# GRU steps 64 to 495 as PE loops, with the products beside them in fp16

## The reference, cut to what matters

```python
def cell(h, x):                       # 512 steps, one after the other; h is 4 x 512
    gi = x @ W_ih + b_ih              # does not depend on h
    gh = h @ W_hh + b_hh
    i_r, i_z, i_n = jnp.split(gi, 3, axis=-1)
    h_r, h_z, h_n = jnp.split(gh, 3, axis=-1)
    r = jax.nn.sigmoid(i_r + h_r)
    z = jax.nn.sigmoid(i_z + h_z)
    n = jnp.tanh(i_n + r * h_n)
    h_new = (1.0 - z) * n + z * h
    return (h_new, h_new)
...
x = x + _L2_cond_ref(cond_2048, x, L2_cond_W_ih, L2_cond_W_hh, L2_cond_b_ih, L2_cond_b_hh)
x = x + _L3_cond_ref(x, cond_2048, 1, 1)   # each row of x, interpolated at 512 places given by cond
```

## Time and profile before

| | |
|---|---|
| median of 3 runs | 2281.44 us (2278.91 to 2283.96) |
| the profiled execution | 2288.73 us |
| its span, first to last instruction | 2286.8 us |
| busy: PE, DVE, ACT, POOL | 2172.7, 1563.6, 1207.0, 504.3 us |
| steps 64 to 495 begin, end | 952.74, 2228.05 us |
| granted clock in steps 64 to 495 | 1.00 |

### The profile page before, as it was taken

One profiled execution on the slowest core, in us unless ns is written; L12 is line 12 of the kernel. 1 busy time (PEld: TensorE's weight loads), 2 busy tenths in 40 slices (PEclk: granted clock), 3 DMA queues, 4 the chain that ended last, 5 costly groups with the idle time before them and its releaser, 6 DMA issues.

```text
span 2286.8 us, 130730 instructions
## 1 busy us (share of the span) xinstructions
PE 2172.7 (95%) x56269; PEld 1831.7 (80%) x56269; DVE 1563.6 (68%) x6093; ACT 1207.0 (53%) x5574; POOL 504.3 (22%) x2271
## 2 busy tenths in 40 slices
PE   5768999999989999999999999999999999999998
PEld 3654655545545999999999999999999999999997
DVE  7987968869687466666666666666666667666665
ACT  6765947759467344566444444444444444444443
POOL 2002121021211122233222222222222222222222
PEclk8569999999999999999999999999999999999999
DMA  5000000010010000000000000000000000000000
GB/s 204 3 2 1 1 1 1 1 56 1 1 56 1 22 5 5 5 5 5 5 5 9 5 9 10 5 9 5 9 10 5 10 5 9 10 5 14 12 10 15
DMA packets 8715, 31.51 MB, mean 14 GB/s; under 512 B 1028, under 2 KB 1352, under 8 KB 7880
## 3 DMA queue, kind: packets, MB, share of 16 engines
q1 hardware_dynamic: 7712, 23.07, 2.7%
q10 hardware_dynamic: 424, 0.07, 0.0%
HBM read 18.94 MB, written 4.19 MB: 10 GB/s over the span
## 4 chain that ended last, share of the span: by engine, by line
PE 81%; DVE 12%; ACT 4%; issue 2%; DMA 1%; POOL 0%; SPq 0%; DVEq 0%; POOLq 0%; ACTq 0%
PE psum L1924 53%; PE psum L1832 9%; PE psum L1735 3%; PE psum L1656 3%; PE psum L1698 2%; PE psum L1753 2%; PE psum L1859 2%; PE psum L1719 2%; DVE region_cols L1087 2%; DVE region_cols L1103 2%; DVE top L1280 2%; ACT region_rows L751 1%; PE psum L1675 1%; DMA region_cols<-in_L_cond_W_emb_dram 1%; PE psum L1872 1%
## 5 line engine op out<-in xcount | busy, mean ns | idle before, releaser
L1924 PE MATMUL psum<-partsA,region_w_hh 128*128 128x40 f16 x24576 | 858.2, 179 | 7.2 <-issue 1.7
L1924 PE MATMUL psum<-partsB,region_w_hh 128*128 128x40 f16 x24576 | 858.2, 179 | 2.4 <-issue 1.9
L1924 PEld LDWEIGHTS psum<-partsA,region_w_hh 128*128 128x128 f16 x24576 | 761.7, 96 | 82.2 <-DVE partsA L1499 11.3
L1924 PEld LDWEIGHTS psum<-partsB,region_w_hh 128*128 128x128 f16 x24576 | 726.7, 95 | 5.4 <-issue 3.8
L564 POOL TENSOR_TENSOR region_w_b<-region_w_b 128x16 f32<-128x16 f32 x1022 | 242.6, 237 | 1135.5 <-DVE region_w_b L1488 1135.5
L1462 DVE TENSOR_REDUCE psum<-psum 128x8 f32<-128x32 f32 x1024 | 201.2, 197 | 292.5 <-PE psum L1924 291.3
L916 ACT ACTIVATE mixA<-psum 128x8 f32<-128x8 f32 x512 | 94.7, 185 | 549.7 <-DVE psum L1462 549.7
L930 ACT ACTIVATE region_w_b<-psum 128x8 f32<-128x8 f32 x1024 | 189.3, 185 | 151.2 <-DVE psum L1477 94.1
L1832 PE MATMUL psum<-region_cols,region_w_a 128*128 128x256 f32 (+1 forms) x864 | 252.7, 390 | 1.0 <-DVE region_cols L1269 0.9
L1488 DVE TENSOR_TENSOR_SCAN region_w_b<-giveB,region_w_b 128x40 f32<-128x40 f32 x512 | 123.6, 241 | 128.5 <-ACT region_w_b L930 128.5
L566 POOL COPY region_work<-region_w_b 128x8 f32<-128x8 f32 x1024 | 203.5, 199 | 2.2 <-DVE region_w_b L1488 2.2
(11 more groups left out here) (234 smaller groups left out, 2590.3 us busy)
## 6 DMA issues: line engine op xcount, KB each, us to landing
region_rows<-in_x_dram SPq DMA_DIRECT2D x4, 1024.0 KB, 11.1
region_w_a<-in_L_cond_W_qkv_dram SPq DMA_DIRECT2D x1, 3072.0 KB, 22.9
region_w_hh<-in_L_cond_W_hh_dram SPq DMA_DIRECT2D x4, 768.0 KB, 6.5
region_w_a<-in_L_cond_W_ih_dram SPq DMA_DIRECT2D x1, 3072.0 KB, 10.2
out_dram<-region_w_b SPq DMA_DIRECT2D x12, 256.0 KB, 3.1
region_cond<-in_cond_dram SPq DMA_DIRECT2D x2, 1024.0 KB, 7.9
region_cols<-in_L_cond_W_emb_dram SPq DMA_DIRECT2D x1, 2048.0 KB, 19.4
region_w_out<-in_L_cond_W_out_dram SPq DMA_DIRECT2D x1, 1024.0 KB, 21.5
```

Source lines behind the costliest of these rows:

```text
L1924: made = e.matmul(k.slots(bank)[:, :, ch, :, 0:2], k.w16[:, 2 * read + c, part, NC * "rzn".index(g) + 2 * half + ch], k.parts[read][:, c]. ...
```

## The change

From step 64 on, PE's code is a loop over steps (`Fori`) for each stretch of 8, 16 or 48 steps of one kind: 23 loops, each aligned to a block of 256 instructions. Inside, the values that semaphores must reach are registers, and the four side matmuls of a turn find their operands by register addresses, which `lower_ap` works out ahead of the units `BAr` and `ABz`.

Each side operand is split into two fp16 parts, as the state is: `w_parts` and `x_parts` for the gates, `x3_parts` and `sampling` for the rows. One fp32 matmul of 256 columns becomes four fp16 matmuls of 256 columns. ACT makes each high part and DVE the low one, in steps given by tables (`W_STEPS`, `X_STEPS`, `HAT_STEPS`, `X3_STEPS` and others), after DVE has found scales of 2 from the largest weights and inputs (`dve_input_most` in steps 0 to 27, `dve_input_scale` in 28 to 33). POOL's addition of the diagonal to the hats goes to DVE.

All groups of the loops go to one bank, with products that always add to what is there; ACT takes a group after its last turn and then writes zeros into the bank (`act_clear`), and PE waits for `cleared` before each turn's side products. PE no longer waits for `zsum` and `nline`. The gates of steps 0 to 127 stay in fp32.

```diff
-    for i in range(ROW_GROUPS * B):
-        plan.append((LATE_PRODUCTS + NC * i, [("late", i)], 1))
...
+def loop_groups():
+
+    groups = []
+    for q in range(2, CHUNKS):
+        s = STARTS[q]
+        if q + 1 < CHUNKS:
+            groups += [("gates", s + NC * j, q + 1, j) for j in range(12)]
+            s += 12 * NC
+        if q > 2:
+            groups += [("rows", s + NC * i, 4 * (q - 3) + turn) for i, turn in enumerate(ROW_TURNS)]
+    for second in range(2):
+        groups += [("late", LATE_PRODUCTS + NC * (4 * second + i), 4 * second + turn) for i, turn in enumerate(ROW_TURNS)]
+    return groups
+
+
+LOOPED = STARTS[2]
+LOOP_GROUPS = loop_groups()
+LOOP_GROUP_AT = {group[1]: n for n, group in enumerate(LOOP_GROUPS)}
+TAKE_STEPS = {group[1] + NC - 1: n for n, group in enumerate(LOOP_GROUPS)}
+CLEARED = [group[1] + NC for group in LOOP_GROUPS]
...
+def act_take_looped(e, k, n):
+    s = k.sem
+    kind, _, *args = LOOP_GROUPS[n]
+    e.wait_ge(s["side_products"], NC * (n + 1))
+    if kind == "gates":
+        act_take_gates(e, k, *args, SIDE_BANK[0], None)
+    elif kind == "rows":
+        act_take_rows(e, k, *args, SIDE_BANK[0])
+    else:
+        act_take_late_rows(e, k, *args, SIDE_BANK[0])
+
+
+def act_clear(e, k, n):
+    s = k.sem
+    kind, _, *args = LOOP_GROUPS[n - 1] if n else ("gates", 0, 2, 10)
+    if kind == "gates":
+        e.wait_ge(s["gates_in"], 12 * args[0] + args[1] + 1)
+    else:
+        e.wait_ge(s["rows_out"], ROWS_TAKEN[n - 1])
+    e.activation(k.bank(SIDE_BANK[0], HALF_ROW), k.zero[:].broadcast_to([P, HALF_ROW]),
+                 ACT.Copy).then_inc(s["cleared"], CLEARED[n] - (CLEARED[n - 1] if n else 0))
...
+        if st in TAKE_STEPS:
+            act_take_looped(e, k, TAKE_STEPS[st])
+            if TAKE_STEPS[st] + 1 < len(LOOP_GROUPS):
+                act_clear(e, k, TAKE_STEPS[st] + 1)
+        if st == LOOPED - 4:
+            act_clear(e, k, 0)
+        if st in W_STEPS:
+            act_weight_high(e, k, W_STEPS[st])
+        if st in X_STEPS:
+            act_input_high(e, k, *X_STEPS[st])
+        if st in AWAY_STEPS:
+            act_away(e, k, AWAY_STEPS[st])
         if st in HAT_STEPS:
             act_hat(e, k, HAT_STEPS[st])
+        if st in HAT_HIGH_STEPS:
+            act_hat_high(e, k, HAT_HIGH_STEPS[st])
+        if st in X3_STEPS:
+            act_x3_high(e, k, X3_STEPS[st])
...
+def dve_input_low(e, k, q, c):
+    s = k.sem
+    e.wait_ge(s["x_halved"], NC * (q - FIRST_HALVED) + c + 1)
+    e.scalar_tensor_tensor(k.x_parts[:, q % 2, 1, c], k.xT[:, c, :, STARTS[q]:STARTS[q] + LONG], k.in_scale[:, 1:2],
+                           k.x_parts[:, q % 2, 0, c], ALU.mult, ALU.subtract).then_inc(s["x_lowered"], 1)
...
+        if st < MOST_PIECES:
+            dve_input_most(e, k, st)
+        if SCALE_AT <= st < SCALE_AT + len(SCALE_OPS):
+            dve_input_scale(e, k, st - SCALE_AT)
+        if st - 1 in W_STEPS:
+            dve_weight_low(e, k, W_STEPS[st - 1])
         if st in PLACE_STEPS:
             dve_place(e, k, PLACE_STEPS[st])
+        if st in X_LOW_STEPS:
+            dve_input_low(e, k, *X_LOW_STEPS[st])
+        if st in DIAGONAL_STEPS:
+            dve_diagonal(e, k, DIAGONAL_STEPS[st])
+        if st in HAT_LOW_STEPS:
+            dve_hat_low(e, k, *HAT_LOW_STEPS[st])
         if st in ADDS:
             dve_add_states(e, k, *ADDS[st])
+        if st in X3_LOW_STEPS:
+            dve_x3_low(e, k, *X3_LOW_STEPS[st])
+        if st in NEXT_LOW_STEPS:
+            dve_next_low(e, k, NEXT_LOW_STEPS[st])
...
+            dve_last_low(e, k, c - 1)
+    dve_last_low(e, k, NC - 1)
...
+def pe_four_batches(e, k, bank, parts, part, c):
+
+    for low in range(2):
+        for sampled in range(2):
             for b in range(B):
-                made = e.matmul(k.bank(part, HALF_ROW)[32 * b:32 * b + 32], k.xT[:, c, b, rows],
-                                k.sampling[:, b, c, part * HALF_ROW:(part + 1) * HALF_ROW],
-                                start=(c == 0), stop=(c == NC - 1), tile_position=(0, 32 * b))
-        made.then_inc(s["last_rows"], 1)
+                made = e.matmul(k.bank(bank, HALF_ROW)[32 * b:32 * b + 32], parts[:, c, low, b],
+                                k.sampling[:, part, b, c, sampled],
+                                start=(c == low == sampled == 0), stop=(c == NC - 1 and low == sampled == 1), tile_position=(0, 32 * b))
+    return made
...
+    for st in range(LOOPED):
+        pe_step(e, k, st)
+        pe_side(e, k, st)
+    for q in range(2, CHUNKS):
+        at = STARTS[q]
+        if q + 1 < CHUNKS:
+            pe_gate_loop(e, k, q + 1)
+            at += 12 * NC
+        if q == 2:
+            pe_free_loop(e, k, at, STARTS[3])
+        else:
+            tile, second = divmod(q - 3, 2)
+            for half in range(ROW_GROUPS):
+                pe_row_loop(e, k, at + 2 * NC * half, B * tile + 2 * second, half)
+    for second, half in itertools.product(range(2), range(ROW_GROUPS)):
+        pe_row_loop(e, k, LATE_PRODUCTS + 2 * NC * (2 * second + half), B * (NT - 1) + 2 * second, half)
+    for st in range(NEXT_PRODUCTS, S):
+        pe_step(e, k, st)
+        pe_side(e, k, st)
...
+def pe_gate_loop(e, k, q):
+    s = k.sem
+    first = STARTS[q - 1]
+    w_parts = k.w_parts.rearrange("p j c l n -> p (j c l n)")
+    x_parts = k.x_parts[:, q % 2].rearrange("p l c b n -> p (l c b n)")
+    if q > FIRST_HALVED:
+        e.wait_ge(s["x_lowered"], NC * (q - FIRST_HALVED + 1))
+    e.addr_align(PE_BLOCK, max_nops=4)
+    with e.Fori(0, 12 * NC) as turn:
+        weights = [w_parts[:, bass.ds(turn * (2 * P) + low * P, P)] for low in range(2)]
+        moving = [x_parts[:, bass.ds(turn % NC * HALF_ROW + low * NC * HALF_ROW, HALF_ROW)] for low in range(2)]
+        count = e.compute_val(turn + (first + 1))
+        e.compute_val(turn % NC)
+        pe_looped_step(e, k, count, weights, moving)
+        if q == FIRST_HALVED:
+            e.wait_ge(s["w_lowered"], W_PIECES)
+            e.wait_ge(s["x_lowered"], NC)
+        pe_looped_products(e, k, count, weights, moving)
...
+    sampling = k.sampling[:, half, b:b + 2].rearrange("p b c l n -> p (b c l n)")
+    e.wait_ge(s["x3_lowered"], 2 * (u + 2))
+    e.wait_ge(s["hat_lowered"], 2 * NC * (b + 2))
+    e.addr_align(PE_BLOCK, max_nops=4)
+    with e.Fori(0, 2 * NC) as turn:
+        weights = [x3_parts[:, bass.ds(turn * (2 * P) + low * P, P)] for low in range(2)]
+        moving = [sampling[:, bass.ds(turn * (2 * HALF_ROW) + low * HALF_ROW, HALF_ROW)] for low in range(2)]
+        count = e.compute_val(turn + (first + 1))
+        pe_looped_step(e, k, count, weights, moving)
+        pe_looped_products(e, k, count, weights, moving)
...
+def pe_looped_step(e, k, count, weights, moving):
+    for u in GRU_UNITS:
+        if u == "BAr":
+            e.lower_ap(weights[0], for_matmul_weights=True)
+            e.lower_ap(moving[0])
+        if u == "ABz":
+            e.lower_ap(weights[1], for_matmul_weights=True)
+            e.lower_ap(moving[1])
+        pe_unit(e, k, u, count)
+
+
+def pe_looped_products(e, k, count, weights, moving):
+    s = k.sem
+    to = k.bank(SIDE_BANK[0], HALF_ROW)
+    e.wait_ge(s["cleared"], count)
+    for stationary in weights:
+        for columns in moving:
+            made = e.matmul(to, stationary, columns, start=False, stop=True, skip_group_check=True)
+    made.then_inc(s["side_products"], 1)
...
+    if u in ("AAr", "BAr"):
+        e.wait_ge(s[f"low{u[0]}"], count)
+    if u in ("AAr", "ABr"):
+        e.wait_ge(s[f"put{h}"], count)
```

More of the change, by code:

```diff
@@ L140 @@
 SIDE = side_table()
-BANK_USE = [("gates", 0, j) for j in range(12)] + [group for _, groups, _ in side_plan() for group in groups]
 def side_done(s):
     return [(group, number % 2) for group, number, part in SIDE.get(s, ()) if part[-1] == NC - 1]
-FREE = [st for st in range(2 * LONG) if st >= LONG and not side_done(st)]
-PLACE_STEPS = {st: i for i, st in enumerate(range(44, 44 + 3 * B))}
-HAT_STEPS = {st: i for i, st in enumerate(FREE[:2 * B * NC])}
-def add_table():
[L156 to L165, removed]
+FIRST_HALVED = 3
@@ new lines, in pe_free_loop @@
+def pe_free_loop(e, k, first, end):
+    e.addr_align(PE_BLOCK, max_nops=4)
+    with e.Fori(first + 1, end + 1) as count:
+        for u in GRU_UNITS:
+            pe_unit(e, k, u, count)
[7 more added lines that the diff above has]
+            e.lower_ap(moving[1])
+        pe_unit(e, k, u, count)
@@ new lines, in pe_step, with pe_unit @@
+def pe_step(e, k, st):
+    s = k.sem
+    if st == 0:
+        e.wait_ge(s["gru_first"], 16)
+        e.wait_ge(s["w_kept"], NC)
+        e.wait_ge(s["w_low"], NC)
+    for u in GRU_UNITS:
+        pe_unit(e, k, u, st + 1)
+def pe_unit(e, k, u, count):
+    s = k.sem
+    read, h, g = "AB".index(u[0]), u[1], u[2]
+    half = "AB".index(h)
+    bank = {"r": R_BANK, "z": Z_BANK, "n": N_BANK}[g][half]
+    if u in ("AAr", "BAr"):
+        e.wait_ge(s[f"low{u[0]}"], count)
```

(22 more changed lines are left out.)

377 lines of the change are left out of this document (242 added, 135 removed).

## The result

The changed kernel takes 2250.21 us (median of 4 runs, 2247.79 to 2251.07) against 2282.7 us before (4 runs, 2278.91 to 2288.22): ratio 0.9854, 95% interval 0.9832 to 0.9876. That is 32.5 us less where 41 were forecast; the forecast of 2240 was 10 us too low.

A forecast was written before the change was run, and what follows sets the result against it. PE was taken to set the step's pace, near a 2.805 us floor. 33 + 14.5 saved less 5 + 1 + 1 makes 41 us: profiled 2288.73 to 2248, median 2240; own range 2223 to 2260, overall 2222 to 2348.

The forecast's parts named there:

- Side products: In 416 steps, four fp16 matmuls replace one fp32 matmul on PE: step 2.923 to 2.84 us, 33 us saved.
- Instruction fetch: In steps 64 to 495, PE's waits for the next code block vanish because loops stay within one block: 14.5 us saved.
- Entries: PE entering each of 23 loops in a new code block: 0.2 us each, 5 us given back, range 0 to 23.
- Loop control: PE's added waits, register computations and branch in each turn: hidden behind queued work, costing nothing.
- Rival A: PE's sequencer becomes the bound: at 80 ns an instruction, 108 us over 432 turns, giving 2348 us; chance 0.18.
- the cluster: About 14 control instructions around a loop's end on PE: 0.71 us at 51 ns each, hidden by 0.87 us.
- Rival B: The backward branch drops the code block, so every turn fetches again: 86 us, giving 2326 us; chance 0.08.
- Clear: ACT's zeroing of 256 columns behind the take in 104 steps: fits its 1.20 us gap, cost 0; 10 us if doubled.
- halves' work: ACT's fp16 copies and DVE's low parts fit idle gaps; with the input search in steps 0 to 27, 1 us.
- The end: After the recurrent steps, the last sums gain a pass through ACT and DVE before PE may start: 1 us added.

The follow-up runs named there:

- written-out code: The changed kernel with its 23 loops written out, constant addresses and waits, fp16 side matmuls kept: 2281.8 us, ratio 1.0007 to the kernel before.
- the loop of four blocks: The changed kernel with four steps in each loop turn instead of one, about 840 instructions: 2288.13 us, ratio 1.0026 to the kernel before.

## Why the prediction came out right, and 10 us low

- *Side products*, 33 us: right. 416 x (2.923 - 2.842) = 33.7 us in loops. What the sum did not say is that they gain nothing in written-out code.
- *Instruction fetch*, 14.5 us: the right cause, and mis-sized. From the medians the kernel before has 2282.7 - 2239.55 - 33.7 = 9.5 us of stalls, if nothing else differs; I took them from one execution that lay 7 us over the median, as the prediction itself noted, and left that difference in the term.
- *Entries*, 23 x 0.2 = 5 us: the step that failed. They cost 10.7 us by the medians and 7.8 by the traces. The nearest row, DVE's 41 ns, was the wrong one: PE's branch over the padding takes 304. The range, 0 to 23, held it.
- So: -33.7 - 9.5 + 10.7 = -32.5, what was measured; but 9.5 and 10.7 are both taken from the same medians, so this sum had to close. The traces alone split it otherwise: stalls of 14.5 and 12 us before, entries of 7.8, windows 39 to 41 us apart. That they come near the 41 us of the forecast proves little: the two traces of before lie 6 and 1 us over its median, that of the changed kernel 2.4 under its own, and what lies outside the window takes 1010.9 to 1015.9 us over all traces here. How the missing 8.5 us divide between fetch and entries is not settled.
- *Loop control*, nothing: right, with 0.13 to 0.19 us of room where 0.87 - 0.71 = 0.16 was worked out, though the prices were mixed (208 for the branch back, 32 for an addition). Rival A was near: three more instructions cost 60 us. (Its 108 us counted all 432 turns; the 16 of the free loop lack the cluster, so 104.) The Trainium skill (Advanced Engine Details and Errata, Control Flow Timing) gives a compare-and-branch about 108 ns; these traces say 208 taken and 76 not.
- *Rival B*: no packet per turn, in none of the loops; the loop of four blocks kept them all, and the written-out code was 42 us slower than loops without alignment (45 by the ratios). The Trainium skill (Runtime: NRT & Kernel Launch, Instruction fetch mechanics) says that a taken branch out of a window of two blocks forces a fetch, and names that as a reason to unroll, while the same section gives PE room for 2048 instructions, eight blocks. The four-block loop agrees with the eight and not with the two, and here unrolling lost.
- *Clear* and *halves' work*, 0 and 1 us: the clear leaves ACT 0.35 us before mixA in the step shown, and without alignment the window is what its steps need, so neither costs anything from step 64 on. Steps 0 to 63, where the 1 us was put, take 192.6 to 193.4 us in the runs of the change whose loops are unaligned or written out, for 192.0 and 192.4 before: 1 us fits.
- *The end*, 1 us: not shown by this pair. From the last recurrent product to the span's end there are 10.7 us against 10.9; but 9.4 in the other trace of before and 10.7 to 13.1 in the other runs of the change.

## What to carry to other kernels

Where long straight code feeds an engine, count its instructions per us: shortening the work makes the next block late, and the gain can vanish. A loop brings it back, and in this kernel its control was free as long as queued work covered it; work out that cover and keep the entry free of a branch to new code. Read a stall term from several executions, or correct it by how far the profiled one lies from the median.

## What had not been expected

- Alignment of a loop to a block, meant to save fetches, cost 7 to 11 us: 304 ns a branch with loops of one block, 2.2 us at most row loops of four. Without it the loops had 131 packets and 0.1 us of stalls.
- A cut of 0.2 us in the time that a block of code lasts (3.82 to 3.62 us) came with a rise of the stalls from 10 to 35 us in the profiled executions.
- A stall comes more from a packet that starts late than from a long one. In the written-out code, where a block start stalled by more than 0.2 us, the block's packet began 1.37 us (median) after the block ahead of it did, and took 1.15 us; where nothing stalled, 1.03 and 0.97. What delays a packet stays open: no run separated the causes.
